# One attention and MLP kernel on one core: another order of statistics, input turns and residual at the end of each batch

## The chip, the cores and the metric

The kernel runs on one core of one Trainium2 chip. The metric is the device time of one execution in microseconds. A core has five engines that work side by side and wait for each other through semaphores: TensorE (PE, matrix products and transposes; PEld is its weight load), VectorE (DVE), ScalarE (ACT), GpSimd (POOL), and SyncE (SP), which here only issues transfers. Each engine takes its own instructions in order.

## The reference

The input x has 4 batches of 2048 rows of 512 values. Two layers follow each other, each with a residual and a layer norm behind it.

1. Attention: x is normalised per row and scaled by gamma and beta; q, k and v are products with a 512x512 weight each; causal softmax of q k^T / sqrt(512) times v, times an output weight; the layer adds its input twice (its own residual and the outer one) and a layer norm gives x1.
2. A mixture of 8 experts that share one MLP: h = silu(silu(x1 w1) w3) w2; a softmax over x1 wr gives each row's two best experts, whose normalised gates scatter rows of gate times h into the output's first 8 rows; everything else of the layer is x1 itself, and a last layer norm gives the output.

```
x = layernorm(x + attention(x)); x = layernorm(x + ffn(x))
out = out.at[indices_k[:, k]].add(gates[:, k:k + 1] * h)   # indices are expert numbers 0..7
```

All products are in single precision, built from rounded high and low parts: a product is three matmuls (high x high, high x low, low x high).

## The kernel before, in words

**Stages.** First the weights are folded (q's with k's into m, v's with the output weight into wvo). Then comes attention, batch by batch, and last the MLP in 16 groups of 512 rows of x1, which go through a scratch in DRAM.

**Attention.** A batch has 16 tiles of 128 rows, in groups of 4. Keys come in chunks of 512, so tile 15 has 4 chunks. For each group of 4 tiles, two pairs of input tiles are loaded into `xin` (ACT issues the loads), normalised (`norm_x`: DVE computes mean and variance, POOL turns them into scale and shift, ACT applies them) and transposed by TensorE in four units (`turn_x`, two per pair, units 0 to 3). Each unit goes through one PSUM bank, `XBANK`: ACT copies it out with gamma and beta into `affine`, and DVE splits it into high and low parts (`split_x`). Unit n+1 may enter the bank when ACT has read unit n. With all four units there, `project_g` makes the group's G product (x times m) and `project_v` its v. Of tile t, `attend` multiplies the transposed probabilities of a chunk with v into the bank `ATTN`; `residual` on DVE (line 952) then reads that bank, scales it by the row sum and adds the doubled residual in `tok`. TensorE may start the next tile's first chunk when this is done (`attn_read`). Tiles 8 to 14 (`FAR`) have their probabilities transposed through DRAM; TensorE transposes the others.

**Behind a tile.** `norm_behind(b, t)` makes two layer norms in one: that of tile t (giving x1) and that of tile t-1 (giving the output). DVE's part is the statistics (lines 884 and 888), POOL's the scale and shift, ACT's the two normalisations (line 633). SP then stores tile t's x1 and tile t-1's output. `tok` has 4 slots; a slot is loaded again when its output is stored.

**The order.** It is written out by hand, one function `tile` per engine. The loop runs over batches 0 to 2; the last batch is written out separately with `last=True`. The next batch's first two pairs of inputs and their four turns are done in tiles 14 and 15 of the batch before. In tile 14, DVE does tile 13's `norm_behind` first, then the split of unit 1, then the statistics of the second pair; behind them, in tile 15, stands tile 14's `residual`. In tile 15, TensorE turns units 2 and 3 ahead of the first and ahead of the second chunk. In the last batch there is no next input. There `xin` takes w1 and w3, which ACT and DVE split (`split_w13`, lines 699 and 967) in tiles 11 to 14, and in tile 15 DVE transposes the MLP's first group of x1 (`turn_x1`, line 1076) between the splits of chunks.

**SP's queue** isn't touched by the change. At each tile it loads `tok`, stores x1 of tile t-2 (line 417) and the output of tile t-3 (line 421). Behind the last tile it issues the loads of the MLP's first two groups (line 357):

```
            for t in range(3, TILES):
                tile(B - 1, t)
            sp.wait_ge(scores_ready, B * CHUNKS)
            ...
            for i in range(2):
                load_x1(sp, i, i * GROUP * P)
```

The line numbers here and in the rows are those of the kernel before.

Of the kernel before, what the change touches and what calls it, by code (L numbers as in the profile page):

```python
# [30 lines left out]
P = 128  # L31
# [9 lines left out]
def attention_mlp(nc, x, wq_t, wk_t, wv_t, wo, gamma, beta, w1_t, w3_t, w2_t, wr_t, out):  # L41

    B, S = 4, x.shape[0] // 4
    TILES = S // P
# [4 lines left out]
    def chunks(t):  # L49

        return t // GROUP + 1
# [24 lines left out]
    with ExitStack() as whole:  # L76
# [69 lines left out]
        TURN0 = 4  # L146
        ATTN = 6
        XBANK = 7


        consts_memset = sem("consts_memset")
# [332 lines left out]
        def _(pool):  # L484
# [39 lines left out]
            def tile(b, t, last=False, before=True):  # L524

                g, k = t // GROUP, t % GROUP
                pool.wait_ge(res_loaded[t % SLOTS], (b * USES + t // SLOTS + 1) * DMA)
                y = tok[:, t % SLOTS, :]
                pool.tensor_tensor(y, y, y, ALU.add).then_inc(res_doubled, 1)
                if k == 3 and g + 2 < GROUPS:  # L530
                    norm_x(b, 2 * (g + 2))
                if k == 3 and g + 2 == GROUPS and not last:
                    norm_x(b + 1, 0)
                if t:
                    norm_behind(b, t - 1, z=2 if before or t > 1 else 1)
                elif before:
                    norm_behind(b - 1, TILES - 1)
                if t == TILES - 1 and not last:
                    norm_x(b + 1, 2)
                if k == 0 and g + 1 < GROUPS:  # L540
                    norm_x(b, 2 * (g + 1) + 1)
                if t == TILES - 2 and not last:
                    norm_x(b + 1, 1)

            def batch(b, last):
                for t in range(PEELED, TILES):
# [46 lines left out]
        def _(act):  # L593
# [16 lines left out]
            def turn_x(b, g, u, more=True):  # L610

                n = g * XUNITS + u
                act.wait_ge(xt_ready, 1 + b * (GROUPS * XUNITS) + n)
                act.wait_ge(x_turned, b * (GROUPS * XUNITS) + n + 1)
                for k in range(2):
                    c = 2 * (u % 2) + k
                    last = act.activation(affine[:, 256 * k:256 * (k + 1)], psum[:, XBANK, 256 * k:256 * (k + 1)],
                                          ACT.Identity, bias=beta_sb[:, c:c + 1], scale=gamma_sb[:, c:c + 1])
                last.then_inc(affine_ready, 1)
                if u % 2 == 1 and more:  # L620

                    if n // 2 + 1 < TILES // 2:
                        load_x(b, n // 2 + 1)
                    else:
                        load_x(b + 1, 0)
# [75 lines left out]
            def tile(b, t, last=False, before=True):  # L701
# [14 lines left out]
                    turn_x(b + 1, 0, 0)  # L716
                if t == TILES - 1 and not last:
                    turn_x(b + 1, 0, 2)
                if more and k == 1:
                    norm_x(b, 2 * (g + 1) + 1)  # L720
                for c in range(max(chunks(t), n_next)):
# [19 lines left out]
                    norm_x(b, 2 * (g + 2))  # L741
                if k == 3 and g + 2 == GROUPS and not last:
                    norm_x(b + 1, 0)
                if t and not (t == TILES - 1 and not last):
                    norm_behind(b, t - 1, (0, 1) if before or t > 1 else (0,))
                if t == TILES - 2 and not last:
                    norm_x(b + 1, 1)
# [10 lines left out]
                    norm_behind(b - 1, TILES - 1)  # L758

                from_tile = TILES - 1 - GROUP  # L760
                if last and from_tile <= t < TILES - 1:
                    split_w13(2 * (t - from_tile))
                if last and from_tile - 1 <= t < TILES - 2:
                    if t >= from_tile:
# [85 lines left out]
        def _(dve):  # L850
# [119 lines left out]
            def tile(b, t, last=False, before=True):  # L970
                g, k = t // GROUP, t % GROUP
                more = g + 1 < GROUPS
                if t:
                    residual(b, t - 1)
                early_maxima = range(chunks(t + 1) - 1) if t + 1 < TILES else range(0)
                for c in early_maxima[0:1]:
                    chunk_max(b, t + 1, c)
                if t in FAR:
                    turn_probs(b, t, 0)
                for c in early_maxima[1:]:  # L980
                    chunk_max(b, t + 1, c)
                if t != TILES - 1:
                    split_probs(b, t, 0)
                if t in FAR:
                    turn_probs(b, t, 1)
                if more and k == 0:
                    split_x(b, g + 1, 0)
                if t + 1 < TILES:
                    row_bias(b, t + 1)
                row_sum(b, t)  # L990
                if chunks(t) > 1:
                    split_probs(b, t, 1)
                if more and k == 0:
                    split_x(b, g + 1, 1)
                if more and k == 2:
                    split_x(b, g + 1, 2)
                if t == TILES - 2 and not last:
                    split_x(b + 1, 0, 0)
                if t == TILES - 1 and not last:
                    split_x(b + 1, 0, 2)  # L1000
                if t in FAR:
                    for c in range(2, chunks(t)):
                        turn_probs(b, t, c)
                        split_probs(b, t, c)
                if k == 3 and g + 2 < GROUPS:
                    norm_x(b, 2 * (g + 2))
                if k == 3 and g + 2 == GROUPS and not last:
                    norm_x(b + 1, 0)
                if t:
                    norm_behind(b, t - 1, z=2 if before or t > 1 else 1)  # L1010
                elif before:
                    norm_behind(b - 1, TILES - 1)
                if t + 1 < GROUP:
                    split_v(b, t + 1)
                if t == TILES - 2 and not last:
                    split_x(b + 1, 0, 1)
                if t == TILES - 1 and not last:
                    split_x(b + 1, 0, 3)
                if t == TILES - 1 and last:
                    dve.wait_ge(x1_loaded[0], LOADS)  # L1020
                    turn_x1(0, 0)
                    turn_x1(0, 1)
                if chunks(t) > 2 and t not in FAR:
                    split_probs(b, t, 2)
                if t == TILES - 1 and last:
                    turn_x1(0, 2)
                    turn_x1(0, 3)
                if t == TILES - 1 and not last:
                    split_g(b + 1, 0)
                if chunks(t) > 3 and t not in FAR:  # L1030
                    split_probs(b, t, 3)
                if t == TILES - 2:
                    split_probs(b, TILES - 1, 0)
                if t == TILES - 1 and last:
                    split_wr()
                if more and k == 2:
                    split_x(b, g + 1, 3)
                    split_v(b, GROUP * (g + 1))
                    split_g(b, g + 1)
                    for j in range(1, GROUP):  # L1040
                        split_v(b, GROUP * (g + 1) + j)
                if more and k == 0:
                    norm_x(b, 2 * (g + 1) + 1)
                if t == TILES - 2 and not last:
                    norm_x(b + 1, 1)
                from_tile = TILES - 1 - GROUP
                if last and from_tile <= t < TILES - 1:
                    split_w13(2 * (t - from_tile))
            def batch(b, last):
                at_batch[0] = b  # L1050
# [167 lines left out]
        def _(pe):  # L1218
# [13 lines left out]
            def turn_x(b, g, u):  # L1232

                n = g * XUNITS + u
                if u % 2 == 0:
                    pe.wait_ge(x_normed, b * (TILES // 2) + n // 2 + 1)
                pe.wait_ge(affine_ready, 1 + b * (GROUPS * XUNITS) + n)
                for k in range(2):
                    c = 2 * (u % 2) + k
                    for tile in range(2):  # L1240
                        at = 256 * k + P * tile
                        last = pe.transpose(psum[:, XBANK, at:at + P], xin[:, tile, c * P:(c + 1) * P], ident[:])  # L1242
                last.then_inc(x_turned, 1)

            def project_g(b, g, first=False):
# [79 lines left out]
            def tile(b, t, last=False, before=True):  # L1325
# [17 lines left out]
                    turn_x(b, g + 1, 2)  # L1343
                if t == TILES - 2 and not last:
                    turn_x(b + 1, 0, 0)
                if t == TILES - 1 and not last:
                    turn_x(b + 1, 0, 2)
                if t + 1 < GROUP:
                    project_v(b, t + 1)
                for c in range(chunks(t)):  # L1350
                    if c + 1 < chunks(t):
                        turn_probs(b, t, c + 1)
                    elif t == TILES - 2:
                        turn_probs(b, TILES - 1, 0)
                    if more and k == 2 and c == chunks(t) - 1:
                        turn_x(b, g + 1, 3)
                    if c == 1 and t == TILES - 2 and not last:
                        turn_x(b + 1, 0, 1)
                    if c == 1 and t == TILES - 1 and not last:
                        turn_x(b + 1, 0, 3)  # L1360
                    attend(b, t, c)
                    if c == 1 and t == TILES - 1 and not last:
                        project_g(b + 1, 0)
                    if c == 2 and t == TILES - 1 and not last:
                        score(b + 1, 0, 0)
# [141 lines left out]
```

## Time and profile before

| | |
|---|---|
| time, median of 3 runs | 1663.91 us (1661.66 to 1664.42) |
| the profiled execution | 1662.27 us |
| its span, first to last instruction | 1660.5 us |
| TensorE, matmuls busy | 1626.9 us (98%), 7615 matmuls |
| VectorE busy | 879.6 us (53%) |
| ScalarE busy | 681.2 us (41%) |
| GpSimd busy | 284.5 us (17%) |
| mean granted TensorE clock | 0.994 |

Times of instructions are in microseconds from the first instruction of the span. A row of the timeline has the start, the duration, the engine, the line, the operation, what it writes and reads, their shapes and a count. An engine name with a q (ACTq, SPq) is its queue that issues transfers. Brackets at the end hold how long the engine was idle before the row, and what ended that. Matmuls overlap: each is shown some 0.39 us long while one of 512 columns starts every 0.23 us. The granted clock is the share of the full TensorE clock of 2.4 GHz; 0.50 is 1.2 GHz.

### The profile page before, as it was taken

To read this page: it belongs to the slowest core of one execution; us is meant where nothing else is said; L and a number is where in the kernel's file an instruction comes from. 1 tells how busy PE (TensorE), PEld (TensorE's weight loads), DVE (VectorE), ACT (ScalarE), POOL (GpSimd) and SP (SyncE) were. 2 spreads that over 40 slices of the span, in tenths; PEclk is the share of its full clock that TensorE was granted. 3 is DMA by queue.
4 is the path that set the end of the run, shared out by engine and by line. 5 is a ranking of instruction groups with operands and counts; after the bars stand their busy time and mean duration, and the time that the engine had idled before them with its cause. 6 is when DMAs were issued, how large, how long until landed. Compare 5 with 4: busy or idle time off the path is not lost.

```text
span 1660.5 us, 23631 instructions
## 1 busy us (share of the span) xinstructions
PE 1626.9 (98%) x7615; PEld 1344.8 (81%) x7615; DVE 879.6 (53%) x2264; ACT 681.2 (41%) x1301; POOL 284.5 (17%) x491
## 2 busy tenths in 40 slices
PE   9999999899999989999999999999989999999998
PEld 7888888788888878888887788888878888888886
DVE  5464645455364554556455455555555655556553
ACT  5443433353343344343333335333344444454443
POOL 1121101121120112121110112020131212212121
PEclk9999999999999999999999999999999999999999
DMA  4111625321153431124534122253663313133100
GB/s 159 58 64 53 156 78 137 86 93 54 59 139 96 118 105 64 64 89 106 131 88 115 51 83 102 77 137 95 156 135 56 51 25 51 28 48 48 27 0 8
DMA packets 365766, 136.64 MB, mean 82 GB/s; under 512 B 317008, under 2 KB 321104, under 8 KB 365664
## 3 DMA queue, kind: packets, MB, share of 16 engines
q1 hardware_dynamic: 354768, 116.48, 28.2%
q10 hardware_dynamic: 10896, 18.90, 3.4%
q8 instruction: 53, 0.87, 0.2%
q14 instruction: 49, 0.40, 0.1%
HBM read 79.73 MB, written 55.59 MB: 81 GB/s over the span
## 4 chain that ended last, share of the span: by engine, by line
PE 55%; issue 33%; POOL 5%; ACT 3%; DVE 2%; DMA 1%; SPq 0%; POOLq 0%; ACTq 0%; DVEq 0%
PE psum L346 17%; PE psum L348 16%; PE psum L347 16%; POOL rstd L507 2%; ACT tok L633 1%; PE psum L1306 1%; ACT xin L633 1%; PE psum L1242 1%; PE psum L1422 1%; PE psum L1421 1%; PE psum L1414 1%; PE psum L1413 1%; POOL expo L582 1%; POOL shift L509 1%; DVE stats L884 1%
## 5 line engine op out<-in xcount | busy, mean ns | idle before, releaser
L346 PE MATMUL psum<-xt_hi,g_hi 128*128 128x512 f32 (+3 forms) x640 | 237.4, 371 | 0.4 <-DVE g_lo L910 0.4
L348 PE MATMUL psum<-xt_lo,g_hi 128*128 128x512 f32 (+3 forms) x640 | 229.6, 359 | 0.0
L347 PE MATMUL psum<-xt_hi,g_lo 128*128 128x512 f32 (+3 forms) x640 | 229.2, 358 | 0.0
L346 PE MATMUL psum<-v_hi,pt_hi 128*128 128x512 f32 x544 | 222.9, 410 | 4.9 <-DVE tok L952 3.2
L347 PE MATMUL psum<-v_hi,pt_lo 128*128 128x512 f32 x544 | 215.2, 396 | 0.0
L348 PE MATMUL psum<-v_lo,pt_hi 128*128 128x512 f32 x544 | 215.1, 395 | 0.0
L504 POOL TENSOR_TENSOR var_eps<-meanvar,eps 128x2 f32<-128x2 f32 (+1 forms) x97 | 19.3, 199 | 1025.9 <-DVE meanvar L888 1023.6
L933 DVE TENSOR_REDUCE rowmax<-psum 128x1 f32<-128x512 f32 (+3 forms) x160 | 97.0, 607 | 149.1 <-PE psum L348 147.8
L808 ACT ACTIVATE act_f<-psum 128x512 f32<-128x512 f32 x128 | 76.6, 598 | 209.7 <-PE psum L348 209.7
L633 ACT ACTIVATE tok<-tok,shift,rstd 128x512 f32<-128x512 f32 x128 | 97.4, 808 | 99.7 <-POOL shift L509 99.4
L582 POOL TENSOR_TENSOR expo<-euler,shifted 128x32 f32<-128x32 f32 x16 | 86.9, 5432 | 297.8 <-DVE shifted L1145 297.8
L346 PEld LDWEIGHTS psum<-xt_hi,g_hi 128*128 128x128 f32 x640 | 121.1, 189 | 16.8 <-DVE g_lo L910 0.5
L688 ACT ACTIVATE pt_hi<-pt_f 128x512 fp32r<-128x512 f32 (+2 forms) x96 | 55.4, 578 | 191.3 <-DVE pt_f L929 190.7
L347 PEld LDWEIGHTS psum<-xt_hi,g_lo 128*128 128x128 f32 x640 | 120.7, 189 | 15.9
L348 PEld LDWEIGHTS psum<-xt_lo,g_hi 128*128 128x128 f32 x640 | 120.3, 188 | 15.9
L346 PEld LDWEIGHTS psum<-v_hi,pt_hi 128*128 128x128 f32 x544 | 103.9, 191 | 31.5 <-DVE pt_lo L921 6.7
L348 PEld LDWEIGHTS psum<-v_lo,pt_hi 128*128 128x128 f32 x544 | 103.6, 191 | 23.1
L347 PEld LDWEIGHTS psum<-v_hi,pt_lo 128*128 128x128 f32 x544 | 104.0, 191 | 18.8
L910 DVE TENSOR_TENSOR g_lo<-psum,g_hi 128x512 fp32r<-128x512 f32 x64 | 44.3, 692 | 131.4 <-ACT g_hi L630 131.4
L671 ACT ACTIVATE probs<-psum,bias 128x512 f32<-128x512 f32 (+3 forms) x157 | 97.2, 624 | 27.8 <-DVE bias L940 12.4
L914 DVE TENSOR_TENSOR v_lo<-psum,v_hi 128x512 fp32r<-128x512 f32 x64 | 44.1, 688 | 119.6 <-ACT v_hi L655 119.6
L346 PE MATMUL psum<-wvo_hi,h_hi 128*128 128x512 f32 x256 | 101.5, 397 | 0.2 <-DVE h_lo L1134 0.2
(150 smaller groups left out, 3410.5 us busy)
## 6 DMA issues: line engine op xcount, KB each, us to landing
xin<-in_x ACTq DMA_DIRECT2D x64, 256.0 KB, 2.8
tok<-in_x SPq DMA_DIRECT2D x64, 256.0 KB, 2.7
x_scratch<-tok SPq DMA_DIRECT2D x64, 256.0 KB, 2.2
out_dram<-tok SPq DMA_DIRECT2D x64, 256.0 KB, 2.3
p_scratch<-probs SPq DMA_DIRECT2D x64, 256.0 KB, 2.0
probs<-p_scratch SPq DMA_DIRECT2D x256, 64.0 KB, 2.6
x_in<-x_scratch SPq DMA_DIRECT2D x64, 256.0 KB, 4.1
p_scratch<-probs SPq DMA_DIRECT2D x16, 192.0 KB, 1.9
```

The costliest lines, as they stand in the source:

```text
L346: pe.matmul(o, ws, ms, start=first, stop=False, skip_group_check=True)
L347: pe.matmul(o, w_lo, ms, start=False, stop=False, skip_group_check=True)
L348: return pe.matmul(o, ws, m_lo_, start=False, stop=last, skip_group_check=True)
L507: pool.tensor_tensor(rstd[:, a:z], var_eps[:, a:z], minus_half[:, o], ALU.pow).then_inc(rooted, 1)
L582: pool.tensor_tensor(expo[:], euler[:], shifted[:], ALU.pow).then_inc(exp_ready, 1)
L633: return act.activation(o, y, ACT.Identity, bias=shift[:, slot:slot + 1], scale=rstd[:, slot:slot + 1])
L671: act.activation(probs[:, at:at + w], psum[:, c, 0:w], ACT.Exp, bias=bias[:, t % 2:t % 2 + 1], scale=SCALE, accum_out=sums4[:, t % 2, c:c ...
L688: act.activation(pt_hi[:, n % 2, 0:w], turned_, ACT.Copy).then_inc(pt_hi_ready, 1)
L808: act.activation(act_f[:, n % 2, :], psum[:, bank, :], ACT.Silu)
L910: dve.tensor_tensor(g_lo[:, j, :], psum[:, j, :], g_hi[:, j, :], ALU.subtract).then_inc(g_ready, 1)
L914: dve.tensor_tensor(v_lo[:, tile, :], psum[:, turn_bank(v_use(tile)), :], v_hi[:, tile, :], ALU.subtract).then_inc(v_ready, 1)
L933: return dve.tensor_reduce((rowmax if chunks(t) == 1 else rowmax4)[:, c:c + 1], psum[:, c, 0:width(t, c)], AX.X, ALU.max)
```

## The change

Four things change at the end of a batch, on POOL, ACT, DVE and TensorE.

1. The second input pair's statistics and normalisation (`norm_x(b + 1, 1)`) stand in tile 14 where tile 13's `norm_behind` stood. Tile 13's `norm_behind` moves to tile 15, directly ahead of or around the turns, and tile 14's follows in tile 15. The last batch moves them too, and with them the last `split_w13` from tile 14 to tile 15.
2. DVE's split of unit 1 moves from tile 14 to tile 15, so that tile 14's `residual` is the first thing behind the split of tile 15's first chunk.
3. TensorE turns units 2 and 3 one chunk later: ahead of and behind chunk 1 of tile 15.
4. Unit 1 of group 1, which is turned in tile 0, goes into PSUM bank 2, and TensorE doesn't wait for ACT's copy of unit 0 there.

```diff
+        SPARE = 2
+        def x_bank(g, u):
+            return SPARE if g == 1 and u == 1 else XBANK
...
# POOL, tile
+                if t == TILES - 2 and not last:
+                    norm_x(b + 1, 1)
+                if t == TILES - 1:
+                    norm_behind(b, t - 2)
-                if t:
+                if t and t != TILES - 2:
                     norm_behind(b, t - 1, z=2 if before or t > 1 else 1)
...
-                if t == TILES - 2 and not last:
-                    norm_x(b + 1, 1)
# ACT, tile
                 if t == TILES - 1 and not last:
                     turn_x(b + 1, 0, 2)
+                if t == TILES - 1 and last:
+                    split_w13(2 * (GROUP - 1))
+                if t == TILES - 1:
+                    norm_behind(b, t - 2)
...
-                if t and not (t == TILES - 1 and not last):
+                if t and t != TILES - 2 and not (t == TILES - 1 and not last):
                     norm_behind(b, t - 1, (0, 1) if before or t > 1 else (0,))
...
-                if last and from_tile <= t < TILES - 1:
+                if last and from_tile <= t < TILES - 2:
                     split_w13(2 * (t - from_tile))
# DVE, tile (the same for its split_w13)
                 if t == TILES - 1 and not last:
+                    split_x(b + 1, 0, 1)
+                if t == TILES - 1 and last:
+                    split_w13(2 * (GROUP - 1))
+                if t == TILES - 1:
+                    norm_behind(b, t - 2)
+                if t == TILES - 1 and not last:
                     split_x(b + 1, 0, 2)
...
-                if t:
+                if t == TILES - 2 and not last:
+                    norm_x(b + 1, 1)
+                if t and t < TILES - 2:
                     norm_behind(b, t - 1, z=2 if before or t > 1 else 1)
...
-                if t == TILES - 2 and not last:
-                    split_x(b + 1, 0, 1)
                 if t == TILES - 1 and not last:
                     split_x(b + 1, 0, 3)
+                if t == TILES - 1:
+                    norm_behind(b, t - 1)
...
-                if t == TILES - 2 and not last:
-                    norm_x(b + 1, 1)
# TensorE, turn_x
-                pe.wait_ge(affine_ready, 1 + b * (GROUPS * XUNITS) + n)
+                if x_bank(g, u) == XBANK:
+                    pe.wait_ge(affine_ready, 1 + b * (GROUPS * XUNITS) + n)
# TensorE, tile
-                if t == TILES - 1 and not last:
-                    turn_x(b + 1, 0, 2)
...
                 for c in range(chunks(t)):
+                    if c == 1 and t == TILES - 1 and not last:
+                        turn_x(b + 1, 0, 2)
                     if c + 1 < chunks(t):
                         turn_probs(b, t, c + 1)
...
+                    attend(b, t, c)
                     if c == 1 and t == TILES - 1 and not last:
                         turn_x(b + 1, 0, 3)
-                    attend(b, t, c)
-                    if c == 1 and t == TILES - 1 and not last:
                         project_g(b + 1, 0)
```

## Rows read from the trace of the kernel before

**Rows 1.** TensorE's waits: who waited, for whom; total us, times, longest.
```profile
PE psum L1242 <- ACT xin L633: 12.5, 3, 4.2
...
PE psum L346 <- DVE tok L952: 3.2, 1, 3.2
```

**Rows 2.** Timeline of TensorE at the first change of batch.
```profile
313.23 0.39 PE L348 MATMUL psum<-v_lo,pt_hi 128*128 128x512 f32 x1
317.78 0.79 PE L1242 MATMUL psum<-ident,xin 128*128 128x128 f32 x4 [4.17 <-ACT xin L633]
...
323.09 0.60 PE L1306 MATMUL psum<-ident,probs 128*128 128x128 f32 x4
...
323.88 0.48 PE L346 MATMUL psum<-v_hi,pt_hi 128*128 128x512 f32 x1
...
326.70 0.39 PE L346 MATMUL psum<-xt_hi,m_hi 128*128 128x512 f32 x1
```

**Rows 3.** Timeline of TensorE at the second and third changes of batch.
```profile
612.02 0.39 PE L348 MATMUL psum<-v_lo,pt_hi 128*128 128x512 f32 x1
...
626.39 0.39 PE L346 MATMUL psum<-xt_hi,m_hi 128*128 128x512 f32 x1
...
911.88 0.39 PE L348 MATMUL psum<-v_lo,pt_hi 128*128 128x512 f32 x1
...
926.50 0.39 PE L346 MATMUL psum<-xt_hi,m_hi 128*128 128x512 f32 x1
```

**Rows 4.** Stretches: length, busy time of PE, PEld, DVE, ACT, POOL, granted clock, DMA.
```profile
318.20:321.50 3.30, 3.30 (x13) 2.82 (x11) 1.10 (x2) 1.51 (x3) 0.00 (x0) 0.50 0.23 74
...
915.60:922.30 6.70, 5.86 (x18) 5.00 (x19) 2.89 (x5) 2.22 (x5) 0.15 (x1) 0.50 0.13 40
```

**Rows 5.** Timeline of VectorE at the first change of batch.
```profile
309.93 1.28 DVE L884 BATCH_NORM_STATS2 stats<-tok 128x6 f32<-128x512 f32 x2
...
311.41 0.39 DVE L902 CAST xt_hi<-affine 128x512 fp32r<-128x512 f32 x1
311.84 0.71 DVE L904 TENSOR_TENSOR xt_lo<-affine,xt_hi 128x512 fp32r<-128x512 f32 x1
312.47 0.68 DVE L921 TENSOR_TENSOR pt_lo<-psum,pt_hi 128x512 fp32r<-128x512 f32 x1
...
314.55 0.72 DVE L952 SCALAR_TENSOR_TENSOR tok<-psum,rinv,tok 128x512 f32<-128x512 f32 x1
```

**Rows 6.** Timeline of ScalarE and its transfers at the first change of batch.
```profile
306.13 0.34 ACTq L608 DMA_DIRECT2D xin<-in_x  x1
...
313.42 1.52 ACT L633 ACTIVATE tok<-tok,shift,rstd 128x512 f32<-128x512 f32 x2 [1.18 <-POOL shift L509]
...
320.04 1.02 ACT L617 ACTIVATE affine<-psum,beta_sb,gamma_sb 128x256 f32<-128x256 f32 x2
```

**Rows 7.** The page's transfers: count, KB each, median us to landing.
```profile
xin<-in_x ACTq DMA_DIRECT2D x64, 256.0 KB, 2.8
```

**Rows 8.** Timeline of TensorE in tile 0, second turn of group 1.
```profile
349.79 0.60 PE L1242 MATMUL psum<-ident,xin 128*128 128x128 f32 x4
```

**Rows 9.** Timeline of SyncE's transfers in the last batch's tile 15.
```profile
1212.23 0.33 SPq L421 DMA_DIRECT2D out_dram<-tok  x1
1212.75 11.30 SPq L357 DMA_DIRECT2D x_in<-x_scratch  x8
```

**Rows 10.** Timeline of VectorE in the last batch's tiles 14 and 15.
```profile
1207.60 1.28 DVE L884 BATCH_NORM_STATS2 stats<-tok 128x6 f32<-128x512 f32 x2
...
1221.14 1.30 DVE L1076 STREAM_TRANSPOSE x1t_f<-x_in 128x512 f32<-128x512 f32 x2 [3.97 <-DMA x_in<-x_scratch]
```

**Rows 11.** Timeline of ScalarE in the last batch, copies of w3.
```profile
1212.11 1.13 ACT L699 ACTIVATE wvo_hi<-xin 128x512 fp32r<-128x512 f32 x2
```

**Rows 12.** Timeline of TensorE in the last batch's tiles 14 and 15.
```profile
1210.93 0.60 PE L1306 MATMUL psum<-ident,probs 128*128 128x128 f32 x4
...
1223.08 0.50 PE L346 MATMUL psum<-v_hi,pt_hi 128*128 128x512 f32 x1
```

More of the change, by code:

```diff
@@ L533, in tile @@
                     norm_x(b + 1, 0)
-                if t:
+                if t == TILES - 2 and not last:
[3 more added lines that the diff above has]
+                if t and t != TILES - 2:
                     norm_behind(b, t - 1, z=2 if before or t > 1 else 1)
-                elif before:
+                elif t == 0 and before:
                     norm_behind(b - 1, TILES - 1)
@@ L616, in turn_x @@
                     c = 2 * (u % 2) + k
-                    last = act.activation(affine[:, 256 * k:256 * (k + 1)], psum[:, XBANK, 256 * k:256 * (k + 1)],
+                    last = act.activation(affine[:, 256 * k:256 * (k + 1)], psum[:, x_bank(g, u), 256 * k:256 * (k + 1)],
                                           ACT.Identity, bias=beta_sb[:, c:c + 1], scale=gamma_sb[:, c:c + 1])
@@ L1008, in tile @@
                     norm_x(b + 1, 0)
-                if t:
+                if t == TILES - 2 and not last:
+                    norm_x(b + 1, 1)
+                if t and t < TILES - 2:
                     norm_behind(b, t - 1, z=2 if before or t > 1 else 1)
-                elif before:
+                elif t == 0 and before:
                     norm_behind(b - 1, TILES - 1)
@@ L1043, in tile @@
                     norm_x(b, 2 * (g + 1) + 1)
-                if t == TILES - 2 and not last:
-                    norm_x(b + 1, 1)
                 from_tile = TILES - 1 - GROUP
-                if last and from_tile <= t < TILES - 1:
+                if last and from_tile <= t < TILES - 2:
                     split_w13(2 * (t - from_tile))
@@ L1241, in turn_x @@
                         at = 256 * k + P * tile
-                        last = pe.transpose(psum[:, XBANK, at:at + P], xin[:, tile, c * P:(c + 1) * P], ident[:])
+                        last = pe.transpose(psum[:, x_bank(g, u), at:at + P], xin[:, tile, c * P:(c + 1) * P], ident[:])
                 last.then_inc(x_turned, 1)
```

## The prediction

> **What bounds the kernel now.** The waits of TensorE come first: three waits of 4.2 us for a normalised input pair, and one of 3.2 us for a residual sum [rows 1]. Those are the only long ones, so TensorE's own stream sets the end and a change is worth what it does to the gaps in that stream. The timeline of TensorE then shows where the three are: at the change from one batch to the next, between the last matmul of tile 14 (313.23) and the first input turn of tile 15 (317.78) [rows 2]. The third view is the granted clock: it reads 0.50 (the 1.2 GHz level) from 318.2 to 321.5 and from 915.6 to 922.3, right behind such gaps [rows 4]. A gap is thus paid twice, so I don't sum idle time but take the whole stretch from the last matmul of tile 14 to the first of the next batch's G product. It is 326.70 - 313.23 = 13.47 us at the first change of batch, 626.39 - 612.02 = 14.37 at the second and 926.50 - 911.88 = 14.62 at the third [rows 2, 3].
>
> TensorE is busy 3.30 of 3.30 us at the half clock [rows 4], so its busy share hides that loss. The Trainium skill (Perfetto Trace Analysis, "Identifying the Most-Contended Engine") says the same of the share: matmul occupancy is no measure of distance from the limit. By idle time alone the three boundaries could give back 12.5 us at most; by the stretches above, more.
>
> **The boundaries, part by part.** Before, DVE in tile 14 does tile 13's statistics at 309.93, the split of input unit 1 at 311.41 and the pair's statistics only afterwards, with the residual of tile 14 behind them at 314.55 [rows 5]. After, the pair's statistics stand at 309.93, if its data is there: the second load is issued at 306.13 and takes 2.8 us [rows 6, 7], so it lands near 308.9, 1.0 us early. The statistics are the same instructions on the same sizes, so the chain on POOL and ACT is that of tile 13's: ACT starts at 313.42 and ends at 314.94 [rows 6]. POOL's doubling of tile 15's residual then stands behind this chain as before.
>
> DVE's next work is the split of tile 15's first chunk at 312.47, and then the residual of tile 14, which now waits for TensorE alone. The new stretch, counted from the start of the last matmul of tile 14: that matmul 0.39, the residual 0.72 [rows 2, 5], and 0.09 for the two hand-overs (estimate), so the first chunk of attention starts at 1.20. The four transposes of chunk 1 run inside that time. One chunk takes 326.70 - 323.88 = 2.82, the turn of an input unit and of a chunk together 323.88 - 323.09 = 0.79 [rows 2]. So 1.20 + 2.82 + 0.79 + 2.82 + 0.40 for the last input turn (half of 0.79) = 8.03 us. The remaining idle, about 0.6 us, should leave the clock high; the long low stretches stand behind gaps of 3.2 us and more.
>
> Gains: 13.47 - 8.03 = 5.4, 14.37 - 8.03 = 6.3 and 14.62 - 8.03 = 6.6, in sum 18.4 us. Covers: the pair is needed at 313.23 + 1.20 + 2.82 = 317.25 and is ready at 314.94, 2.3 us early. What is late next is the third unit's split, needed at 313.23 + 8.03 = 321.3. After ACT's 314.94 come its copy of chunk 1 and DVE's split (0.6 + 0.7), unit 1's split 1.14 (311.41 to 312.55), tile 13's statistics 1.5 (309.93 to 311.41), then, as ACT's copy of unit 2 takes 1.02 after 317.9 [rows 5, 6], the split to about 320.1. That leaves 1.1 us. Tile 13's normalisations and tile 14's statistics now stand on ACT and DVE between the turns, ahead of chunk 2's split (about 326.4); the G product covers them. It is 48 matmuls at 0.23 us, 11 us from 321.3 on. SP stores tile 13's x1 and tile 12's output some 7 us later and so loads the next batch's first residual at about 324, wanted beyond 340. The next batch's third pair is loaded about 1.4 us earlier than before, in kernel time. Bounds for the stretch: 7.6 if the residual is quite hidden, 9.5 if the third split is 1.5 us late. The gain lies between 14 and 19.7.
>
> **The second bank.** At tile 0 the second turn starts at 349.79 with no wait [rows 8], so there is nothing to remove: 0, at most 0.1 us for each of four tiles, and no loss, since nobody else uses bank 2 until the next G product.
>
> **The last batch.** Nothing is turned here, but tile 13's statistics move from tile 14 to tile 15 as well, now behind w3's last split. SP's order is not changed: tile 13's x1, tile 12's output (1212.23), and only then the load of the MLP's first x1 (1212.75) [rows 9]. Before, the statistics begin at 1207.60 [rows 10] and the output store follows 4.63 us later, through POOL and ACT. After, the attention of tile 14 ends near 1211.1 (the next transposes issue at 1210.93 [rows 12]); the residual ends at 1211.9, two small sums at 1212.2, chunk 1's split at 1212.9. ACT's two copies of w3 take 1.13 [rows 11] behind the copy of chunk 1, so to 1213.2, and DVE's second split ends at about 1214.0. The statistics then begin 6.4 us late, so the store is at 1218.6 and the load at 1219.15. From its first issue to DVE's first transpose takes 1221.14 - 1212.75 = 8.39 us [rows 9, 10]: 1227.5. Chunk 2's split stands behind that transpose on DVE, so TensorE's third chunk starts at 1223.08 [rows 12] + 6.4 = 1229.5. TensorE gains 2.9 us at its first chunk and waits it all away, 11 us idle instead of 3.2.
>
> Behind the long idle the clock is low again. The low stretch after a resumption cost 3.3 / 2 = 1.7 us at the first boundary; at the third it stood until 922.3, of which about 5.9 us after the gap, 2.9 us [rows 1, 3, 4]. I take 2.3, in the middle. Before, the low clock here was hidden behind the same load, so it isn't given back. The last batch costs 6.4 + 2.3 = 8.7 us; bounds 5 (a load of 7 us, no low clock) and 12 (a load 2 us longer, 2.9 of clock).
>
> The Trainium skill (DMA: Bandwidth & Descriptors, "Bandwidth" and "Latency and other measured facts") gives some 2 us fixed cost and 436 GB/s, by which this load of 1 MB would be there after 4.4 us, as an estimate; the last batch would then cost 2.4 us and the clock. The row's 8.39 decides.
>
> **Sum.** -18.4 + 8.7 = -9.7 us. The profiled execution took 1662.27 us, so 1652.6; the median of the three runs is 1.64 above that, 1663.91 - 9.7 = 1654.2 us.
>
> **The rivals.** A: the load of x1 doesn't hold TensorE in the last batch. Then 1663.91 - 18.4 = 1645.5. For it: DVE idles 3.97 us before the load already, and the profile shows only one execution; against it: SP's queue is in order and the split of chunk 2 stands behind the load on DVE [rows 9, 10]. B: the clock falls at the boundaries although the gap is short. Then the half clock's 1.7 us stay, and with the differences of the stretches 2.6 and 2.9 at the second and third, 7.2 in all: 1661.4. For it: three gaps closely spaced (a residual, a late split); against it: 0.6 us against 4.17. C, the other side: chunk 2's split takes the place of the removed wait. Its chain in series (chunk 1's split, unit 1, tile 13's statistics, POOL and ACT, the copy and split of unit 3, tile 14's statistics) runs from 315 to 326.4. It decides from 321.3 + 11.0 + 0.4 = 332.7 on; the change is slower than before if it ends after 332.7 + 9.7 / 3 = 335.9. If each step waited once more so that the chain took twice its 11.4 us, it would end at 337.8: 5.1 us three times, 1669.5. For it: it crosses three engines with two links that also wait for TensorE; against it: 6.3 us of slack.
>
> **How the numbers follow.** The forecast has 0.77, A 0.09, B 0.08, C 0.06. Under the forecast the bounds run from 1663.91 - 19.7 + 5 = 1649.2 to 1663.91 - 14 + 12 = 1661.9, with its far end unlikely; I give 1648.0 to 1660.0, which leaves out A, C, part of B and that end. About 0.2% (3.3 us) is what a measurement can tell from no change. Faster: A and nearly all of the forecast, 0.83. Same: B and a rest, 0.10. Slower: C and a rest, 0.07.
>
> **What would show it.** In the changed profile: TensorE's waits for the normalised pair are gone, with three of about 0.6 us for the residual in their place, and the clock at 1.00 across the changes of batch. The stretches measure about 8.0. In the last batch TensorE waits some 11 us for chunk 2's split, DVE some 8 us for the load, and the load is issued some 6.4 us later behind the output store. Wrong would be a stretch over 10 us, a wait at chunk 2 in the loop, or no long wait in the last batch.

## The result, and the profile after

The changed kernel takes 1653.63 us (median of 4 runs, 1652.72 to 1654.77); the kernel before, with one more run beside these, 1662.86 us (1661.66 to 1664.42). The ratio is 0.9946 [0.9932, 0.9961], so it is faster by 0.39 to 0.68%. The forecast was 1654.2 us, faster. One execution of one kernel below (e10) had a mean granted clock of 0.85 and took 1799.63 us; that kernel's time and ratio leave it out.

The profiled execution took 1653.48 us, against 1662.27 before. TensorE's share of busy time is 98% in both, so it doesn't tell the two apart:

```profile
span 1651.7 us, 23631 instructions
...
PE 1621.5 (98%) x7615; PEld 1339.9 (81%) x7615; DVE 880.6 (53%) x2264; ACT 680.9 (41%) x1301; POOL 284.5 (17%) x491
```

TensorE's waits after (who, for whom; total us, times, longest):

```profile
PE psum L351 <- DVE pt_lo L932: 11.5, 5, 10.6
PE psum L1260 <- ACT affine L624: 2.9, 5, 0.8
...
PE psum L351 <- DVE tok L963: 1.6, 4, 0.4
```

The three waits for a normalised pair and the long one for a residual [rows 1] are gone. Four of 0.4 us for the residual have come instead, and one of 10.6 us that was not there. So something was won at three places and part of it lost at a fourth. To put sizes on that, the execution is cut at the starts of the G products, which every batch has at the same place:

| stretch | before | after | difference |
|---|---|---|---|
| start to the last G of batch 0 | 214.96 | 214.54 | -0.42 |
| last G of batch 0 to the first of batch 1 | 111.74 | 106.28 | -5.46 |
| the same, batch 1 to 2 | 112.64 | 106.28 | -6.36 |
| the same, batch 2 to 3 | 112.93 | 106.37 | -6.56 |
| inside batches 1, 2 and 3 | 561.27 | 561.68 | +0.41 |
| last G of batch 3 to the MLP's first matmul | 116.77 | 124.47 | +7.70 |
| MLP and end | 430.15 | 432.03 | +1.88 |

The sum is -8.81 us, the difference of the spans.

**The changes of batch.** TensorE's timeline after, the rows that answer to [rows 2, 3]:

```profile
312.76 0.39 PE L353 MATMUL psum<-v_lo,pt_hi 128*128 128x512 f32 x1
312.99 0.60 PE L1324 MATMUL psum<-ident,probs 128*128 128x128 f32 x4
314.00 0.50 PE L351 MATMUL psum<-v_hi,pt_hi 128*128 128x512 f32 x1 [0.41 <-DVE tok L963]
...
316.85 0.60 PE L1260 MATMUL psum<-ident,xin 128*128 128x128 f32 x4
...
320.47 0.60 PE L1260 MATMUL psum<-ident,xin 128*128 128x128 f32 x4
320.82 0.48 PE L351 MATMUL psum<-xt_hi,m_hi 128*128 128x512 f32 x1
...
606.43 0.39 PE L353 MATMUL psum<-v_lo,pt_hi 128*128 128x512 f32 x1
...
614.49 0.48 PE L351 MATMUL psum<-xt_hi,m_hi 128*128 128x512 f32 x1
...
900.10 0.39 PE L353 MATMUL psum<-v_lo,pt_hi 128*128 128x512 f32 x1
...
908.16 0.48 PE L351 MATMUL psum<-xt_hi,m_hi 128*128 128x512 f32 x1
```

From the last matmul of tile 14 to the G product it is 8.06 us three times (320.82 - 312.76, and so on), where it was 13.47, 14.37 and 14.62. The third input turn, at 316.85, has no bracket: its pair was ready. The clock stayed up in this stretch, as it did at the other two (length; busy time of PE, PEld, DVE, ACT, POOL; granted clock; DMA):

```profile
313.00:321.30 8.30, 7.89 (x43) 6.53 (x42) 5.26 (x13) 4.02 (x8) 2.19 (x5) 1.00 0.00 1
```

VectorE's rows show its part in that, against [rows 5]: the statistics of the next input pair stand first, the residual comes as soon as TensorE's sum is there, and tile 13's statistics, which stood here, now come at 316.31 behind it.

```profile
309.46 1.28 DVE L895 BATCH_NORM_STATS2 stats<-xin 128x6 f32<-128x512 f32 x2
...
313.19 0.75 DVE L963 SCALAR_TENSOR_TENSOR tok<-psum,rinv,tok 128x512 f32<-128x512 f32 x1 [0.69 <-PE psum L353]
...
316.31 1.28 DVE L895 BATCH_NORM_STATS2 stats<-tok 128x6 f32<-128x512 f32 x2
...
324.85 0.66 DVE L932 TENSOR_TENSOR pt_lo<-psum,pt_hi 128x512 fp32r<-128x512 f32 x1
```

**The last batch.** SyncE's issues, then VectorE's and TensorE's timelines after, to be laid beside [rows 9, 10, 12]:

```profile
1200.33 0.33 SPq L426 DMA_DIRECT2D out_dram<-tok  x1
1200.86 11.29 SPq L362 DMA_DIRECT2D x_in<-x_scratch  x8
```

```profile
1195.70 1.28 DVE L895 BATCH_NORM_STATS2 stats<-tok 128x6 f32<-128x512 f32 x2
...
1208.88 1.30 DVE L1093 STREAM_TRANSPOSE x1t_f<-x_in 128x512 f32<-128x512 f32 x2 [7.62 <-DMA x_in<-x_scratch]
1210.11 0.65 DVE L932 TENSOR_TENSOR pt_lo<-psum,pt_hi 128x512 fp32r<-128x512 f32 x1
```

```profile
1199.60 0.60 PE L1324 MATMUL psum<-ident,probs 128*128 128x128 f32 x4
...
1210.82 0.80 PE L351 MATMUL psum<-v_hi,pt_hi 128*128 128x512 f32 x1 [10.62 <-DVE pt_lo L932]
...
1219.62 0.49 PE L1438 MATMUL psum<-x1t_hi,wr_s 128*128 128x512 f32 x1 [1.25 <-POOL fold_rows L578]
```

Statistics at 1195.70, output store 4.63 us later (as before: 1207.60 to 1212.23), load right behind it, first transpose 8.02 us after the load's first issue, chunk 2's split behind the transposes, and TensorE's third chunk behind the split. TensorE's label names the split, VectorE's own label the load: the cause lies two engines away from the wait. Of the 8.02 us, 3.78 go by until SyncE issues the fourth of the four loads (256 KB each) that hold the MLP's first group, at 1204.64, and 4.22 until that one lands. The clock fell in the wait, and TensorE came back at 0.50 (the 1.2 GHz level):

```profile
1204.10:1210.80 6.70, 0.00 (x0) 0.00 (x0) 1.92 (x4) 1.36 (x3) 1.34 (x2) 0.50 1.10 174
1210.90:1214.20 3.30, 3.30 (x8) 2.62 (x9) 3.27 (x8) 1.22 (x2) 0.00 (x0) 0.50 1.11 173
```

8 matmuls stand in those 3.30 us, where the full clock lets one start every 0.23 us, about 14.

### The profile page after: what moved, and what is told of

Read it like the earlier page. It is cut to its first block and busy times, and to the rows that moved or that the text cites. A ratio compares the mean times of both kernels' runs of the same rounds, so it can differ in the third digit from the quotient of the medians.

```text
span 1651.7 us, 23631 instructions
## 1 busy us (share of the span) xinstructions
PE 1621.5 (98%) x7615; PEld 1339.9 (81%) x7615; DVE 880.6 (53%) x2264; ACT 680.9 (41%) x1301; POOL 284.5 (17%) x491
```

## The experiments

The theory is that of the prediction: the boundaries give 18.4 us, and the moved statistics cost some 8 in the last batch because SyncE's queue, which was not changed, puts the MLP's first load behind the store that they end in. Ratios are to the kernel before.

**e1_last_as_before**: the last batch keeps its old order, the three changes of batch the new one.

```diff
-                if t == TILES - 1:
+                if t == TILES - 1 and not last:
                     norm_behind(b, t - 2)
...
-                if last and from_tile <= t < TILES - 2:
+                if last and from_tile <= t < TILES - 1:
                     split_w13(2 * (t - from_tile))
```

> The changed kernel, but in the last batch tile 13's statistics and normalisations and w3's last split stay in tile 14, as in the kernel before. Theory (the last batch lost 7.7 us because the load of x1 is queued on SP behind tile 12's output, which came 6.1 us later): the load is again issued about 1.65 us after tile 14's attention, TensorE waits 3.2 us at tile 15's first chunk and not at the third; 7.7 us faster than the changed kernel, about 1645.9 us. Rival (the last batch lost nothing by its order; the 1.9 us at the very end and noise are all): within 2 us of 1653.6.

Measured: 1645.44 us, 0.9899 [0.9884, 0.9914]. The last G product to the MLP takes 117.46 us (124.47 in the changed kernel, 116.77 before), and the wait for the last batch's residual is back:

```profile
PE psum L351 <- DVE tok L961: 4.5, 4, 3.2
```

So the moved order in this one batch cost 124.47 - 117.46 = 7.0 us by the profiles. The medians differ by more, 1653.63 - 1645.44 = 8.2 us; in the profiles the changed kernel also has 1.75 us more in MLP and end (432.03 against 430.28), of which the last section tells.

**e2_load_first**: the new order everywhere, but SyncE issues the load ahead of tile 13's x1 and tile 12's output.

```diff
                 sp.dma_start(tok[:, slot, :], ...)
+                if loads:
+                    sp.wait_ge(scores_ready, B * CHUNKS)
+                    for i in range(SLOTS):
+                        sp.wait_ge(x1_stored[i], 2 * GROUP // SLOTS * DMA)
+                    for i in range(2):
+                        load_x1(sp, i, i * GROUP * P)
...
-                tile(B - 1, t)
...
+                tile(B - 1, t, loads=t == TILES - 1)
```

> The changed kernel, but SP issues the MLP's first loads of x1 ahead of the stores of tile 13's x1 and tile 12's output. Theory (SP's queue order): the load has landed long before DVE wants it, so chunk 2's split waits only for tile 14's statistics, which end 0.45 us after TensorE's wait began plus 1.1 us; two transposes 1.3 and the split 0.65 behind them: TensorE's third chunk starts about 7.5 us earlier, the remaining wait is about 3 us, and the kernel takes 1644.5 to 1646.2 us. Rival (DVE's longer queue in tile 15, the statistics of two tiles, makes the split late): the wait stays near 10.6 us and the time at 1653.6.

Measured: 1645.79 us, 0.9901 [0.9886, 0.9916]. Its SyncE, VectorE and TensorE rows:

```profile
1182.72 11.77 SPq L362 DMA_DIRECT2D x_in<-x_scratch  x8
```

```profile
1195.01 1.28 DVE L896 BATCH_NORM_STATS2 stats<-tok 128x6 f32<-128x512 f32 x2
...
1198.99 1.29 DVE L896 BATCH_NORM_STATS2 stats<-tok 128x6 f32<-128x512 f32 x2 [2.42 <-POOL shift L515]
...
1200.48 1.27 DVE L1094 STREAM_TRANSPOSE x1t_f<-x_in 128x512 f32<-128x512 f32 x2
```

```profile
1202.38 0.79 PE L351 MATMUL psum<-v_hi,pt_hi 128*128 128x512 f32 x1 [2.88 <-DVE pt_lo L933]
```

The load is some 17 us earlier, counted from the last G product, and the transposes no longer wait for it. Tile 13's statistics (1195.01) are as late as in the changed kernel, and the loss is gone: the last G product to the MLP takes 116.79 us, as in the kernel before. So the loss came through the queue. The place of the statistics has a price of its own as well: a wait of 2.88 us is left at the third chunk, with the clock at 0.50 for 3.4 us behind it, where VectorE had to wait for POOL between two tiles' statistics, and e9 below, which differs from e2 in that place alone, takes 4.7 us less. e1 has its wait of 3.2 us at the first chunk and e2 this one at the third, so a kernel with neither was to be looked for (e9).

**e3_one_bank**: the second bank taken away.

```diff
-            return SPARE if g == 1 and u == 1 else XBANK
+            return XBANK
```

> The changed kernel without its second bank: unit 1 of group 1 goes into the same bank as the others and waits for the copy of unit 0. Theory (that turn had no wait before): no difference, 1653.6 within 0.7 us. Rival (the turns of tile 0 would have waited once the boundaries are shorter, as those of tile 4 do, 0.69 us each): 0.7 us for each of four batches, 1656.4 us.

Measured: 1654.35 us (1651.87 to 1655.7), 0.9952 [0.9938, 0.9965]. The intervals overlap almost wholly; the bank is worth nothing that can be measured, and in e3's profile the turns of tile 0 at the first change of batch have no wait without it either.

**e4_turns_as_before** and **e5_turns_alone** divide the boundaries' gain. e4 is the changed kernel with TensorE's two turns where they were; e5 is the kernel before with the two turns moved (as in the diff, now on TensorE alone) and nothing else.

```diff
+                if t == TILES - 1 and not last:
+                    turn_x(b + 1, 0, 2)
                 if t + 1 < GROUP:
                     project_v(b, t + 1)
                 for c in range(chunks(t)):
-                    if c == 1 and t == TILES - 1 and not last:
-                        turn_x(b + 1, 0, 2)
...
+                    if c == 1 and t == TILES - 1 and not last:
+                        turn_x(b + 1, 0, 3)
                     attend(b, t, c)
```

> The changed kernel with TensorE's turns of units 2 and 3 where they were before (ahead of the first chunk, and ahead of the second); everything else as changed. Theory: the pair is ready 1.1 us after TensorE ends tile 14, so the first turn waits that long, and the second turn waits some 0.5 us for the copy of unit 2; the G product starts about 1.1 us later at each of the three boundaries than in the changed kernel, without a low clock: 3.3 us slower than the changed kernel, about 1656.9 us. Rival (the later turns are the part that counts): the wait of 4 us with the low clock is back, 1668 us or more.

> The kernel before with one part of the change alone: TensorE turns units 2 and 3 one chunk later (and waits for the residual of tile 14 alone ahead of the first chunk); the order on DVE, POOL and ACT is that of before, one bank. Theory A (what gave the gain is that TensorE no longer stands in order behind the pair's normalisation): the first chunk starts when the residual ends, 315.3 instead of 319.08, the pair is ready at 317.65, before it is wanted, and the stretch is 9.0 us instead of 13.5 to 14.6, so 15.5 us less at the three boundaries and nothing lost in the last batch: about 1647.4 us. Theory B (the earlier statistics and residual on DVE gave the gain): the stretch stays above 12 us with the clock low behind it: 1656 us or more.

Measured: e4 1657.93 us, 0.9969 [0.9958, 0.9981]; e5 1647.08 us, 0.9907 [0.9892, 0.9923]. TensorE in e4, then in e5:

```profile
314.80 0.65 PE L1260 MATMUL psum<-ident,xin 128*128 128x128 f32 x4 [1.05 <-ACT xin L640]
...
319.57 0.66 PE L1260 MATMUL psum<-ident,xin 128*128 128x128 f32 x4 [0.48 <-ACT affine L624]
```

```profile
312.79 0.39 PE L353 MATMUL psum<-v_lo,pt_hi 128*128 128x512 f32 x1
...
314.88 0.50 PE L351 MATMUL psum<-v_hi,pt_hi 128*128 128x512 f32 x1 [1.26 <-DVE tok L957]
...
321.75 0.48 PE L351 MATMUL psum<-xt_hi,m_hi 128*128 128x512 f32 x1
```

With the turns alone (e5) a boundary takes 321.75 - 312.79 = 8.96 us, 0.90 more than with everything. From G to G the three boundaries take 107.22, 107.26 and 107.30 us, so of the 18.4 us the turns alone bring 15.5, as theory A said; the new order of the other engines adds some 2.8 there and takes 7.7 back in the last batch. So e5, a part of the change, beats the whole by 6.5 us. With the order alone (e4) a batch's boundary is some 1.4 us longer than with both (107.7 from G to G against 106.28, where 1.1 more was expected), and the wait of 4 us with the low clock, e4's rival, doesn't come back: either half removes most of the wait, and their gains overlap. The new order of VectorE, GpSimd and ScalarE was tried only as a whole, so what each part of it brings is not shown.

**e6_keep_busy** and **e10_keep_busier** ask what the low clock behind the long wait costs. TensorE does 40, or 46, matmuls of no use in that wait (extra work, whose results are overwritten).

```diff
+                    if c == 2 and t == TILES - 1 and last:
+                        pe.wait_ge(probs_ready, 1 + B * CHUNKS)
+                        for _ in range(KEEP):
+                            pe.matmul(psum[:, 0, :], g_hi[:, 0, 0:P], g_hi[:, 1, :], start=True, stop=True, skip_group_check=True)
```

> The changed kernel with 40 matmuls of no use (512 columns, 0.23 us each, into a score bank that is free) ahead of the last batch's third chunk, which fill some 9 of the 10.6 us that TensorE waits there. They are extra work. Theory (the last batch's cost is 6.1 us of a later load and 1.6 us of low clock behind the wait): the third chunk starts at the same time after tile 14, the clock stays at 1.00, and the MLP starts 1.6 us earlier than in the changed kernel: about 1652.0 us. Rival (the load sets the time behind the third chunk as well, through the first x1 parts): no difference, 1653.6.

> As with 40 matmuls of no use ahead of the last batch's third chunk, but 46, so that some 0.4 us of the wait are left instead of 1.8 us, behind which the clock still fell for 3.4 us. Theory (1.6 us of the last batch's 7.7 are the low clock behind the wait): the clock stays at 1.00 there and from the last G product to the MLP's start takes 122.9 us instead of 124.5 to 124.8. Rival (the time to the MLP's start is set by the x1 parts on ACT and DVE, not by TensorE's clock): 124.5 us again, with the clock high.

Measured: e6 1651.99 us, 0.9935 [0.9921, 0.9948], the number expected and not for the reason expected. 1.79 us of the wait were left and the clock fell behind them; the last G product to the MLP took 124.78 us, no less than 124.47. The profiled execution is shorter only at the end (430.35 us for MLP and end, against 432.03), where the edit does nothing. e6, TensorE and its window:

```profile
1210.83 0.50 PE L351 MATMUL psum<-v_hi,pt_hi 128*128 128x512 f32 x1 [1.79 <-DVE pt_lo L932]
```

```profile
1212.40:1215.70 3.30, 3.30 (x9) 2.60 (x8) 2.84 (x7) 0.25 (x1) 0.00 (x0) 0.50 0.90 183
```

e10 took 1651.01 us, 0.9937 [0.9924, 0.9950]. 1.13 us of the wait were left and the clock stayed at 1.00:

```profile
1211.72 0.50 PE L351 MATMUL psum<-v_hi,pt_hi 128*128 128x512 f32 x1 [1.13 <-DVE pt_lo L932]
...
1218.95 0.49 PE L1444 MATMUL psum<-x1t_hi,wr_s 128*128 128x512 f32 x1 [1.25 <-POOL fold_rows L578]
```

```profile
1210.50:1216.00 5.50, 4.37 (x20) 3.54 (x20) 5.47 (x11) 2.45 (x4) 0.00 (x0) 1.00 1.10 200
```

From the third chunk to the MLP it is 1218.95 - 1211.72 = 7.23 us, against 1219.62 - 1210.82 = 8.80 in the changed kernel. The low clock cost 1.57 us there. The Trainium skill (TensorE: Matmul & The Clock Gate, "HAM oscillation — how this bites in real kernels") reckons half of the time spent at the low clock as lost; half of the 3.3 us in which TensorE worked is 1.65, so the trace agrees. Half of the whole low stretch, 10.24 us here, would not have been right, as TensorE stood still in the rest. How long the low clock goes on behind that wait differs between profiles: in e3, e4 and e8, which have the same order there as the changed kernel, the third chunk to the MLP takes 9.15, 9.09 and 10.03 us, so it cost 1.6 to 2.8 us. In e10's profiled execution the third chunk itself came 0.9 us later, as VectorE's transpose came 9.04 us after the load's first issue instead of 8.02; so the last G product to the MLP took 123.86 us, 0.6 less than in the changed kernel, between the theory's 122.9 and the rival's 124.5.

**e8_bank_at_tile_4** gives tile 4's turn the second bank too, where the changed kernel waits 0.51 to 0.53 us in each batch.

```diff
-            return SPARE if g == 1 and u == 1 else XBANK
+            return SPARE if g in (1, 2) and u == 1 else XBANK
```

> The changed kernel with the second bank for unit 1 of group 2 as well, which is turned in tile 4. Theory (there TensorE does wait for the copy, 0.52 us idle and 0.69 us of start-to-start, once a batch): 2.1 to 2.8 us faster than the changed kernel, 1650.8 to 1651.5. Rival (the next thing TensorE wants there, the split of the first chunk of tile 4, is late by as much): no difference, 1653.6.

Measured: 1653.27 us, 0.9947 [0.9934, 0.9961], no gain. The turn runs without a wait and the next chunk's split is late instead, as the rival said (batch 1, where the turn waited 0.53 us):

```profile
398.80 0.60 PE L1260 MATMUL psum<-ident,xin 128*128 128x128 f32 x4
...
402.10 0.50 PE L351 MATMUL psum<-v_hi,pt_hi 128*128 128x512 f32 x1 [0.42 <-DVE pt_lo L932]
```

**e7_all_together** puts every idea together: in the last batch e2's load, POOL's clearing for the MLP early, tile 14's statistics behind the splits of chunks 2 and 3, and at tile 4 e8's bank.

```diff
+                if t == TILES - 1 and last:
+                    clear_for_mlp()
                 if t == TILES - 1:
                     norm_behind(b, t - 2)
...
-                if t == TILES - 1:
+                if t == TILES - 1 and not last:
                     norm_behind(b, t - 1)
...
                 if t == TILES - 1 and last:
+                    norm_behind(b, t - 1)
                     split_wr()
```

> The changed kernel with SP's first x1 loads ahead of the stores of tile 13 and 12; in the last batch POOL clears the MLP's buffers ahead of tile 13's scale and shift, and DVE does tile 14's statistics behind the splits of chunks 2 and 3; and the second bank at tile 4. Theory (each wait has one cause, and none stands close behind): no wait ahead of the third chunk and no low clock there, so the MLP starts about 12 us earlier than in the changed kernel, and 2.4 us from tile 4: 1639 to 1640 us. Rival (with the load out of the way the MLP's first x1 parts or its buffers are late, after the last chunk): 1643 us or more.

Measured: 1646.13 us, 0.9906 [0.9891, 0.9921]; it missed by 6 us. The waits moved on (who, for whom; total, times, longest):

```profile
PE psum L351 <- DVE pt_lo L937: 3.9, 9, 1.4
...
PE psum L351 <- DVE h_lo L1157: 2.8, 1, 2.8
...
PE psum L1444 <- DVE x1t_lo L1104: 1.6, 1, 1.6
```

The MLP starts 113.92 us after the last G product, but then waits 2.82 us for its first group, with the clock low behind it: MLP and end took 434.83 us.

**e9_best** takes only what had been shown: the load first (e2) and the last batch's statistics where they were (e1), with w3's last split left in tile 15.

> The changed kernel's order at the three boundaries; in the last batch tile 13's statistics and normalisations stay in tile 14 as in the kernel before, w3's last split goes behind the split of chunk 1 in tile 15 as in the changed kernel, and SP issues the first x1 loads ahead of the stores of tiles 13 and 12. Theory (two causes made the last batch wait: the load's place on SP, and tile 13's statistics between chunk 1 and chunk 2 on DVE and ACT): the residual waits 0.4 us as at the boundaries, chunk 2's split is there in time, the wait ahead of the third chunk is under 0.5 us, the clock stays at 1.00 and the MLP starts about 111.7 us after the last G product (124.5 in the changed kernel): about 1640.8 us. Rival (ACT's two normalisations ahead of the copy of chunk 1, or tile 14's statistics, make a chunk late again, as when all parts were put together): a wait of 1 us or more in tile 15 or in the MLP's first group, and 1643 us or more.

Measured: 1642.0 us, 0.9873 [0.9856, 0.9889], the best without extra work. The last G product to the MLP takes 112.05 us (111.7 expected), the third chunk has no wait, and the clock stays at 1.00 until the end of the MLP. TensorE's rows at the residual and at the end:

```profile
1194.72 0.50 PE L351 MATMUL psum<-v_hi,pt_hi 128*128 128x512 f32 x1 [0.41 <-DVE tok L964]
...
1627.64 0.50 PE L1431 MATMUL psum<-h_hi,gates_s 128*128 128x512 f32 x1 [1.45 <-DVE h_lo L1148]
...
1629.11 2.08 PE L1489 MATMUL psum<-fold_rows,acc_sb 128*128 128x128 f32 x8 [0.73 <-ACT acc_sb L855]
```

```profile
1629.10:1632.40 3.30, 3.29 (x10) 2.54 (x11) 0.00 (x0) 1.11 (x4) 0.00 (x0) 0.50 0.00 0
```

**e11_best_busy_end** adds to e9 six and three matmuls of no use (extra work) in those two waits of the end.

```diff
+            keep(6)
             gate(NG - 1, 3)
             pe.drain().then_inc(acc_done, 1)
+            keep(3)
```

> The fastest kernel so far (tile 13's statistics in tile 14 in the last batch, the first x1 loads first) with 6 and 3 matmuls of no use in TensorE's two waits at the very end (1.45 and 0.73 us). They are extra work. Theory (in some executions the clock falls behind these waits and the last products take 1.9 us more; the MLP with the end takes 430.1 to 430.4 us or 432.0 us in the profiles so far): never low there, the MLP with the end takes 430.2 us and the median falls by up to 1.9 us, to 1640 to 1641.5 us, with a smaller spread. Rival (the clock falls there for another reason): low in the profile all the same, or the same median of 1642.0.

Measured: 1639.92 us (1638.95 to 1641.52), 0.9868 [0.9854, 0.9882]. In the profile the clock stays at 1.00 and MLP and end take 430.43 us instead of 431.95:

```profile
1626.00:1633.00 7.00, 6.61 (x24) 3.35 (x22) 0.69 (x2) 1.54 (x5) 0.00 (x0) 1.00 0.00 0
```

The interval overlaps that of e9, so its gain over e9 rests on one profile of each and is not established. The slowest of its four executions (1641.52 us) still has a mean clock of 0.999, so in that one the clock fell somewhere.

## Why the prediction was right

- **The boundaries.** 18.4 us predicted, 18.38 measured. Each step came as written: no wait for the pair, three short ones for the residual (0.41 us; about 0.6 predicted), stretches of 8.06 (8.03). That the whole stretch was taken, and not the waits, is what made it right: the waits alone would have given 12.5 less the new 1.2 us. At the first boundary 4.17 - 0.41 of idle time and half of the 3.3 us at the low clock [rows 4] make 5.4, which is the stretch's 13.47 - 8.06; at the other two, where the clock stayed low for 5.4 and 5.9 us behind the wait, the same sum gives 6.4 and 6.7, against 6.3 and 6.6.
- **What is late next.** The pair was ready at 314.06 and asked for at 316.85. The third unit's split ended at 319.75 for a G product at 320.82, so 1.1 us were left, as predicted. Chunk 2's split began at 324.85, some 7 us before its need; rival C did not come near. Rival B did not either: the clock read 1.00 at all three.
- **The second bank.** 0 predicted; e3 shows no difference.
- **The last batch.** 8.7 predicted, 7.70 measured, and the route was the predicted one; e1 and e2 show it from both ends, which refutes rival A. Two sizes were off. The statistics, the store and the load came 6.5 us later (6.4 forecast). From the last G product to the third chunk it was 109.54 us (1113.54 to 1223.08) and is 115.67 (1095.15 to 1210.82), 6.1 more instead of 6.4; the load took 8.02 us instead of 8.39 (and not 4.4, the estimate that the prediction sets beside it). The low clock cost 1.57 (e10) instead of 2.3: the mean of a short and a long low stretch was taken, and it was a short one. With the 1.6 to 2.8 us that the profiles show for it, 2.3 is not wrong as a mean.
- **Not foreseen**: the +1.88 us in MLP and end. It is not the change's: see the last section. The shown terms make 7.70 - 18.38 = -10.7; with the 1.88 and the +0.41 and -0.42 elsewhere they make the profile's -8.81. So it is in part luck that the medians' difference, -9.2, lies within half a microsecond of the -9.7 of the forecast: the last batch cost 1.0 us less than forecast, and the end nearly 2 us more.

What the prediction missed is not a number but a use: it worked out that the last batch would lose 8.7 us through an untouched queue, and took that as the change's price, when moving one load ahead of two stores removes it (116.79 us from the last G product to the MLP in e2, 116.77 before).

## What to carry to other kernels

When an order is changed inside a loop, price the peeled last iteration by itself: the work that made the new order good (here the next batch's turns) is not there, and what follows the loop may hang on the moved step through a queue that nobody edited. Measure a stall as the stretch between two fixed pieces of work on the bounding engine, not as the idle time in it, since the time at the low clock behind it counts as busy time. And try the parts of a change singly: here one of them was worth more than all together.

## What the runs showed of the hardware

At the end of the kernel the clock falls in some profiles and not in others. TensorE has the same two waits there, 1.45 and 0.73 us, in the profiles of the kernel before, the changed kernel and e9. In e3 and before, nothing follows; in the changed kernel, e2, e4 and e9 the clock reads 0.50 for 3.4 us, and MLP and end take 432.0 us instead of 430.1 to 430.4. The changed kernel, and e3, which differs from it in one bank only:

```profile
1641.00:1644.30 3.30, 3.30 (x9) 1.81 (x8) 0.00 (x0) 1.01 (x4) 0.00 (x0) 0.50 0.00 0
```

```profile
1640.50:1644.50 4.00, 4.00 (x15) 2.34 (x16) 0.00 (x0) 0.95 (x4) 0.00 (x0) 1.00 0.00 0
```

The executions of one and the same kernel differ in the same way: three of e9's four have a mean clock of 0.999 and take 1641.90 to 1642.42 us, the fourth has 1.000 and takes 1640.06. So some 1.9 us of this kernel can come and go from one execution to the next.

The length of a wait alone does not tell whether the clock falls. The same 1.45 and 0.73 us have both outcomes. Of single waits, it fell behind 1.79 us in e6's profile and stayed behind 1.84 us at the start of e8, 1.57 and 1.38 in e7, 1.26 in e5 and 1.13 in e10. And two of e6's five executions have a mean clock of 1.000 and take 1649.98 and 1650.59 us, the other three 0.998 or 0.999 and 1651.99 to 1652.60, so behind that wait too the clock does not seem to fall each time. What decides is left open.
